# Routing the first four batches of the second expert stage inside the linear attention before it

## The chip, the cores and the metric

The program runs on one core of one Trainium2 chip. A core has a matrix engine (TensorE, PE in the rows), a vector engine (VectorE, DVE), an activation engine (ScalarE, ACT) and a general one (GpSimd, POOL), each with its own instruction queue; SyncE (SP) issues DMAs. The engines meet only at semaphores. The metric is the device time of one launch in microseconds, the median of several runs. One execution was also taken by the hardware profiler; every time of an instruction below is from that one.

## What is computed

32 sequences ("batches") of 256 tokens with 128 numbers each go through six stages: feed-forward, gated attention, feed-forward, experts, linear attention, experts. The change touches the last two. Cut to them, the reference is:

```python
# linear attention on layernorm(x), 16 heads of 64
q = elu(x @ Wq) + 1; k = elu(x @ Wk) + 1; v = x @ Wv; g = sigmoid(x @ Wg + bg)
kv = einsum('bhnd,bhne->bhde', k, v)
z = 1 / clip(einsum('bhnd,bhd->bhn', q, k.sum(-2)), 1e-6)
x = x + (einsum('bhnd,bhde->bhne', q * SCALE, kv) * z * g) @ Wo
# experts on layernorm(x): 8 experts, top 2, 76 slots for each expert and batch
logits = x @ router_w + router_b
top, idx = top_k(logits, 2); probs = softmax(top)
pos = running count of the expert among the batch's choices
einp[idx, pos] += x
o = silu((einp @ w_fc + b_fc) * (einp @ w_gate + b_gate)) @ w_proj + b_proj
x = x + 0.5 * sum(probs * o[idx, pos])
```

## The kernel before

All of x stays in SBUF as 64 tiles of 128 tokens, two for each batch. A stage is a block: each engine has a program of its own for it, and no engine begins the next stage before all have ended this one.

**The linear attention** (`lin_stage`, "lin4") is a pipeline of one turn for each batch. A turn of PE applies the heads of batch b (`apply_heads`, L1271), transposes them (L1287) and projects them out (L1295), and between these pieces does the keys (K, L1221), the products of rows and keys (XK, L1229), the queries (Q, L1240), the gates (G, L1248) and the keys and values (L1258) of batch b+1, and last the transposes of the normalised batch b+2 (L1214). Turns 0 to 30 are a hardware loop on PE, ACT and POOL; turn 31 is written out. On DVE, turns 0 to 4 are written out (each also adds rows that the expert stage before has left over), the rest are two loops: turns 5 to 27 and 28 to 30. Between the two, DVE works out mean and 1/deviation of batches 0 to 27 for the expert stage to come (`ahead.columns`, L226 to L243, on 56 tiles at once, 17 instructions of which all but two wait for the one before). A turn of DVE is: `normalise` (L261), `divide` 0 and 1 (L1496 to L1501), then key features (L1482), divides and gates (`gate`, L1510) in turn, query features (L1488) and `update` (L1516, L273). PSUM has eight banks: 0 to 3 carry K, XK, Q and G, 4 and 5 the heads and keys, 6 and 7 the transposes, the output and the transposed input.

**The expert stages** (`moe_stage`, "moe3" and "moe5") take the batches in chunks, given by a plan. For a chunk, PE goes through 8 experts, each in 4 steps of two matmuls as wide as the chunk (`up`, L1926 and L1930: 76 columns for each batch), and then one `down` (L1942), which works on blocks of 128 rows, so a chunk of 2 or 3 batches takes 2 blocks for each expert, one of 4 or 5 takes 3. A step is a slot. In the slots of a chunk the batches of the next one are routed: normalise, transpose (L1880), router (L1887), choice and masks on DVE, counts (L1894 to L1898), slots, one-hot rows (first choice on POOL, L1835, second on DVE, L2121), and `send` (L1914), 12 bfloat16 matmuls of 304 columns for each batch. The table `combine_in` says in which slots the results of the chunk before are added to x (L1766); for that POOL gathers them row by row with indirect DMAs (`gather_rows`, L1757, four for each batch), after the stores of that chunk have landed (`rows_kept`). The last chunk's rows are gathered after its last store; in moe3 they are left to the turns of lin4, in moe5 the program ends with them (`combine`, then `store`).

What differs between the two expert stages is the start. moe3 has its first chunk, of four batches, already routed: the feed-forward stage before it does this in its turns (class `RouteAhead`, whose table of lags says in which turn each step of a batch comes), so that PE begins with `up` at once. moe5 routes its first chunk, of two batches, itself, before the first slot (`in_front`), with 16 transposes of the identity on PE (`stay_warm`, L1949) ahead of the sends. The plans are:

```python
FIRST_PLAN = Plan((4, 5, 5, 5, 5, 5, 3), ...)
LAST_PLAN = Plan((2, 3, 5, 5, 5, 5, 5, 2), ...)
```

## Time and profile before

| | us |
|---|---|
| median of 3 runs | 2365.43 (2365.0 to 2366.44) |
| the profiled execution | 2363.26 |
| its span, first to last instruction | 2361.2 |
| moe3, first to last expert matmul | 498.10 to 985.36 |
| lin4, loop turn | 24.70 each |
| between lin4's last matmul and moe5's first expert matmul | 1806.15 to 1822.68 |
| moe5, first to last expert matmul | 1822.68 to 2342.23 |
| from there to the end of the span | 19.0 |

The page of the profile has PE busy 95% of the span, DVE 66%, ACT 54% and POOL 32%; the mean granted clock of PE is 0.986 of full speed. A busy matmul in a row lasts until its results are through, so that following ones overlap: what one costs is read from start to start. "Idle ... <-X" is the engine's pause before an instruction and what ended it.

### The profile page before, as it was taken

To read this page: it belongs to the slowest core of one execution; us is meant where nothing else is said; L and a number is where in the kernel's file an instruction comes from. 1 tells how busy PE (TensorE), PEld (TensorE's weight loads), DVE (VectorE), ACT (ScalarE), POOL (GpSimd) and SP (SyncE) were. 2 spreads that over 40 slices of the span, in tenths; PEclk is the share of its full clock that TensorE was granted. 3 is DMA by queue.
4 is the path that set the end of the run, shared out by engine and by line. 5 is a ranking of instruction groups with operands and counts; after the bars stand their busy time and mean duration, and the time that the engine had idled before them with its cause. 6 is when DMAs were issued, how large, how long until landed. Compare 5 with 4: busy or idle time off the path is not lost.

```text
span 2361.2 us, 45474 instructions
## 1 busy us (share of the span) xinstructions
PE 2241.9 (95%) x14426; PEld 1780.2 (75%) x14426; DVE 1563.1 (66%) x5019; ACT 1277.0 (54%) x2619; POOL 756.0 (32%) x848
## 2 busy tenths in 40 slices
PE   5989998999999999899999999999998989999996
PEld 4979987977777777776777777777776876777776
DVE  6967777876776776556655656656566666767755
ACT  4755545754444444465566666666653444444443
POOL 0402122534676665500000000000001556666754
PEclk9999999999999999999999999999999999999998
DMA  7040000000111111200000000000000001111122
GB/s 266 0 170 0 0 0 1 2 7 24 36 39 40 36 39 47 53 3 0 0 0 0 0 0 0 0 0 0 0 0 1 19 24 35 41 53 48 41 57 76
DMA packets 70833, 68.13 MB, mean 29 GB/s; under 512 B 9520, under 2 KB 58160, under 8 KB 70320
## 3 DMA queue, kind: packets, MB, share of 16 engines
...
q10 hardware_dynamic: 1344, 2.16, 0.3%
q8 instruction: 61, 1.00, 0.2%
...
## 4 chain that ended last, share of the span: by engine, by line
PE 48%; DVE 4%; issue 3%; ACT 1%; POOL 1%; DMA 0%; ACTq 0%; DVEq 0%; POOLq 0%
PE moe_bank L1942 5%; PE lin_bank L1295 5%; PE lin_bank L1221 5%; PE lin_bank L1229 5%; PE lin_bank L1248 5%; PE lin_bank L1240 5%; PE moe_bank L1926 4%; PE moe_bank L1930 4%; PE lin_bank L1271 4%; PE lin_bank L1287 3%; PE moe_bank L1914 2%; PE lin_bank L1258 1%; POOL all_landed L1757 1%; DVE moe_hot L2121 1%; DVE all_x L1766 0%
## 5 line engine op out<-in xcount | busy, mean ns | idle before, releaser
L2010 ACT ACTIVATE moe_fc<-moe_bank,all_b_fc 128x380 f32<-128x380 f32 (+3 forms) x480 | 254.1, 529 | 299.2 <-PE moe_bank L1926 293.6
L2131 DVE SCALAR_TENSOR_TENSOR moe_act<-moe_bank,all_b_moe_gate,moe_fc 128x380 f32<-128x380 f32 (+3 forms) x480 | 263.7, 552 | 172.8 <-PE moe_bank L1930 102.7
L1942 PEld LDWEIGHTS moe_bank<-all_w_proj,moe_act 128*128 128x128 f32 x2624 | 309.5, 193 | 12.9 <-issue 1.2
L1942 PE MATMUL moe_bank<-all_w_proj,moe_act 128*128 128x128 f32 x2624 | 316.5, 277 | 1.7 <-DVE moe_expert_out L2140 1.0
L1757 POOL DMA_INDIRECT all_landed<-rows_out,all_take_at x256 | 275.9, 1078 | 120.8 <-issue 118.5
L1458 POOL COPY lin_xn_ones<-lin_xn 128x254 f32<-128x254 f32 x32 | 12.8, 399 | 740.2 <-PE lin_bank L1229 739.8
L1835 POOL TENSOR_SCALAR moe_hot<-all_slot_ids,moe_slot 128x608 bf16<-128x608 f32 x116 | 210.8, 1825 | 65.5 <-issue 33.0
L2017 ACT ACTIVATE moe_act<-moe_act 128x760 f32<-128x760 f32 (+3 forms) x240 | 178.1, 742 | 97.1 <-DVE moe_act L2131 97.1
L1362 ACT ACTIVATE lin_neg<-lin_bank 128x512 f32<-128x512 f32 x256 | 151.7, 593 | 106.7 <-PE lin_bank L1221 62.7
L1271 PEld LDWEIGHTS lin_bank<-lin_kv,lin_qT 128*128 128x128 f32 x1024 | 145.3, 192 | 73.9 <-issue 54.2
L1930 PE MATMUL moe_bank<-moe_rowsT,all_w_gate 128*128 128x380 f32 (+2 forms) x512 | 174.4, 422 | 4.2 <-DVE moe_act L2131 4.2
L1926 PE MATMUL moe_bank<-moe_rowsT,all_w_fc 128*128 128x380 f32 (+2 forms) x512 | 177.3, 428 | 0.0
L1926 PE MATMUL moe_bank<-gau_rowsT,all_w_fc 128*128 128x380 f32 (+2 forms) x448 | 171.3, 464 | 1.4 <-ACTq L2022 1.4
L1930 PE MATMUL moe_bank<-gau_rowsT,all_w_gate 128*128 128x380 f32 (+2 forms) x448 | 167.6, 456 | 0.8 <-DVE moe_act L2131 0.8
L1366 ACT ACTIVATE lin_neg<-lin_neg 128x512 f32<-128x512 f32 x256 | 161.0, 630 | 7.9
L1271 PE MATMUL lin_bank<-lin_kv,lin_qT 128*128 128x130 f32 x1024 | 153.9, 278 | 8.6 <-DVE lin_heads L1501 8.3
L1390 ACT ACTIVATE lin_gate_tanh<-lin_bank,all_bg_half 128x256 f32<-128x256 f32 x256 | 103.4, 468 | 108.2 <-PE lin_bank L1248 108.1
L2140 DVE TENSOR_TENSOR moe_expert_out<-moe_bank,all_b_proj 128x384 f32<-128x384 f32 (+1 forms) x120 | 62.4, 520 | 113.4 <-PE moe_bank L1942 103.9
L1221 PE MATMUL lin_bank<-all_wk,lin_xT 128*128 128x512 f32 x256 | 132.2, 621 | 5.0 <-ACT lin_xT L1358 3.3
L1516 DVE TENSOR_TENSOR all_x<-lin_bank,all_x 128x256 f32 (+1 forms) x32 | 13.6, 424 | 179.1 <-PE lin_bank L1295 179.1
L1930 PEld LDWEIGHTS moe_bank<-moe_rowsT,all_w_gate 128*128 128x128 f32 x512 | 93.2, 190 | 48.1 <-DVE moe_act L2131 5.2
L1295 PE MATMUL lin_bank<-all_wo,lin_gated 128*128 128x128 f32 x1024 | 127.8, 278 | 0.8 <-DVE lin_gated L1510 0.8
...
## 6 DMA issues: line engine op xcount, KB each, us to landing
...
all_landed<-rows_out,all_take_at POOLq DMA_INDIRECT x256, 2.9
...
```

Of the source, the lines that this page charges most:

```text
L1221: nc.tensor.matmul(bank[j][:, :], xT[:, j // 2 * P:(j // 2 + 1) * P], k.wk[:, j % 2 * HU:(j % 2 + 1) * HU], start=True, stop=True).then_in ...
L1271: last = nc.tensor.matmul(bank[4 + n % 2][:, i * 2 * DH1:(i + 1) * 2 * DH1], qT[:, p, t * P:(t + 1) * P], kv[:, p, :], start=True, stop=True)
L1295: last = nc.tensor.matmul(bank[6][:, t * DIM:(t + 1) * DIM], gT[:, p, t * P:(t + 1) * P], k.wo[:, p, :], start=(p == 0), stop=(p == PAIRS ...
L1366: nc.scalar.activation(neg[:, j, :], neg[:, j, :], ACT.Exp, scale=-1.0).then_inc(exps.sem, 1)
L1757: nc.gpsimd.indirect_dma_start(landed[:, b % LANDED, t, h, :], None, k.rows_out, bass.IndirectOffsetOnAxis(take_at[:, i, h:h + 1], 0), bou ...
L1835: nc.gpsimd.tensor_scalar(hot[:, b % 2, t, :], k.slot_ids[:, :], slot[:, b % 2, t, 0:1], None, ALU.is_equal).then_inc(hot_first, 1)
L1926: nc.tensor.matmul(bank[FC + j % 2][:, 0:c.width], k.w_fc[:, e, j * P:(j + 1) * P], rowsT[:, c.n % 2, e, 0:c.width], start=True, stop=True ...
L1930: nc.tensor.matmul(bank[GATE + j % 2][:, 0:c.width], k.w_gate[:, e, j * P:(j + 1) * P], rowsT[:, c.n % 2, e, 0:c.width], start=True, stop= ...
L1942: last = nc.tensor.matmul(bank[OUT][:, j * DIM:(j + 1) * DIM], act_in[:, i % 2, h, j * P:(j + 1) * P], k.w_proj[:, e * MC + h, :], start=( ...
L2010: nc.scalar.activation(fc[:, j, 0:c.width], bank[FC + j % 2][:, 0:c.width], ACT.Identity, bias=k.b_fc[:, e * MC + j:e * MC + j + 1]).then_ ...
L2017: nc.scalar.activation(a, a, ACT.Silu).then_inc(act_sb, 1)
L2131: nc.vector.scalar_tensor_tensor(act_in[:, i % 2, j, 0:c.width], bank[GATE + j % 2][:, 0:c.width], k.b_moe_gate[:, e * MC + j:e * MC + j + ...
```

## The change

1. The linear attention gets a `RouteAhead` of its own for four batches. Turns 0 to 15 stay a loop, turns 16 to 30 are written out on every engine. Batch n of the four starts in turn 16 + 3n: normalise, split, transpose in that turn, copy and router one turn later, choice, masks and count two later, slots and first choice three, second choice and first send four, second send five, last landing six. The last piece is ACT's copy in turn 31.
2. In such a turn PE does its part at the end of the turn, after `transpose_x`, in banks 3 and 2, and in the middle of the next turn (`banks_read`) waits that they have been read. DVE reads the banks after `divide` 1 (`read_psum`) and does the rest after `divide` 5 (`on_vector`). ACT copies at the start of a turn; POOL works after its copy of rows. The normalised tile and two others lie in `k.landed`, which is free by then.
3. The scales for batches 0 to 3 are worked out on DVE before turn 16 (8 tiles), those of batches 4 to 27 before turn 28 (48 tiles).
4. moe5 starts like moe3: no `in_front`, no `stay_warm`. Its plan is that of moe3 but for the last chunk, whose results of the chunk before are added in slots 15, 19, 23, 27 and 31. The first chunk's rows are in `k.rows_ahead`, the others in `rowsT`.
5. The weights of the first three stages, `rowsT` of moe3 and other tiles that are no longer needed are given up after moe3, so that the new ones fit.
6. In the feed-forward stage before moe3, two reads of PSUM move from `on_vector` to `read_psum`, called right ahead of it, and signal a semaphore of their own.

```diff
+    def banks_read(self, pe, turn):
+        for what, done, per, g in [("copy0", self.xT_sb, 1, 0), ("choose", self.logits_sb, 1, 0), ("assign", self.counts_sb, 1, 0),
+                                   ("land0", self.sent_sb, 2, 0), ("land1", self.sent_sb, 2, 1)]:
+            n = self.at(what, turn)
+            if n is not None:
+                pe.wait_ge(done, per * n + g + 1)
+
+    def read_psum(self, dve, turn):
+        nc, k = self.nc, self.k
+        n = self.at("choose", turn)
+        if n is not None:
+            dve.wait_ge(self.logits_ps, n + 1)
...
+        n = self.at("assign", turn)
...
@@ lin_stage
+        room = (k.landed[:, 0, :, 0, :], k.landed[:, 0, :, 1, :], k.landed[:, 1, 0, :, :])
+        routing = RouteAhead(k, route, ahead, LINEAR_AHEAD, [(0, 1)], [(0, 4), (4, 8)],
+                             (bank[3][:, 0:SEQ], bank[2][:, 0:TILES * EXPERTS], bank[2][:, 0:TILES * TOP_K * EXPERTS], bank[3]),
+                             k.rows_ahead[:, :, :], room)
...
-                with pe.Fori(0, BATCHES - 1) as b:
+                def turn(b):
...
                     transpose_heads(b, 0)
+                    if isinstance(b, int):
+                        routing.banks_read(pe, b)
                     K(b, 1, 2)
...
                     transpose_x(b, 2)
+                    if isinstance(b, int):
+                        pe.wait_ge(g_sb.sem, g_sb.at(b, 1, 1))
+                        routing.on_tensor(pe, b)
+
+                with pe.Fori(0, LINEAR_FROM) as b:
+                    turn(b)
+                for b in range(LINEAR_FROM, BATCHES - 1):
+                    turn(b)
...
-                with pool.Fori(1, BATCHES) as b:
+                with pool.Fori(1, LINEAR_FROM + 2) as b:
                     copy_rows(b)
+                for b in range(LINEAR_FROM, BATCHES - 1):
+                    if b + 2 < BATCHES:
+                        copy_rows(b + 2)
+                    routing.on_gpsimd(pool, b)
...
                     divide(b, 1)
+                    if routes:
+                        routing.read_psum(dve, b)
...
                     divide(b, 5)
+                    if routes:
+                        routing.on_vector(dve, b)
                     gate(b, 1)
...
-                with dve.Fori(len(k.carried.batches), AHEAD // TILES) as b:
+                with dve.Fori(len(k.carried.batches), LINEAR_FROM) as b:
                     turn(b)
-                dve.wait_ge(stat.sem, stat.at(AHEAD // TILES - 1))
-                ahead.columns(dve, chain, 0, AHEAD)
-                with dve.Fori(AHEAD // TILES, BATCHES - 1) as b:
+                dve.wait_ge(stat.sem, stat.at(route - 1))
+                ahead.columns(dve, chain, 0, TILES * route)
+                for b in range(LINEAR_FROM, BATCHES - 1):
+                    if b == AHEAD // TILES:
+                        dve.wait_ge(stat.sem, stat.at(AHEAD // TILES - 1))
+                        ahead.columns(dve, chain, TILES * route, AHEAD)
                     turn(b)
@@ plans
-LAST_PLAN = Plan((2, 3, 5, 5, 5, 5, 5, 2), (9, 5, 5, 5, 5, 5, 9),
-                 (None, (14, 6), (11, 6), (11, 5), (11, 5), (11, 5), (11, 5), (20, 5)), False)
+LAST_PLAN = Plan((4, 5, 5, 5, 5, 5, 3), (5, 5, 5, 5, 5, 9), (None, (11, 5), (11, 5), (11, 5), (11, 5), (11, 5), (15, 4)))
+LINEAR_FROM = 16
+LINEAR_AHEAD = LINEAR_FROM, 3, {"norm": 0, "transpose0": 0, "split": 0, "copy0": 1, "router": 1, "choose": 2, "mask": 2, "count": 2,
+                                "assign": 3, "first": 3, "hot0": 4, "hot1": 4, "send0": 4, "land0": 5, "send1": 5, "land1": 6}
@@ moe_stage, tensor engine
-                if how.routed_ahead:
-                    for s in (xT_ps, logits_ps, count_ps):
-                        pe.sem_inc(s, OWN)
-                    pe.sem_inc(sent_ps, 2 * OWN)
-                else:
-                    for part in (transpose_x, router, count):
-                        for b in in_front:
-                            part(b)
-                    stay_warm(WARM)
-                for b in in_front:
-                    for h in range(2):
-                        send(b, h)
+                for s in (xT_ps, logits_ps, count_ps):
+                    pe.sem_inc(s, OWN)
+                pe.sem_inc(sent_ps, 2 * OWN)
@@ program
-        lin_stage(k, "lin4")
-        moe_stage(k, "moe5", LAST_PLAN, d["out"])
+            k.rows_ahead = k.sb("rows_ahead", [P, EXPERTS, LAST_PLAN.chunks[0] * CAP])
+            lin_stage(k, "lin4", LAST_PLAN.chunks[0])
+            moe_stage(k, "moe5", LAST_PLAN, d["out"])
```

On PE, between the last matmul of lin4 (L1295) and the first expert matmuls of moe5, there stands before:

```order
L1295 MATMUL lin_bank<-all_wo,lin_gated 128x128 x16
L1198 UNCONDITIONAL_BRANCH
L1872 UNCONDITIONAL_BRANCH
L1880 MATMUL moe_bank<-all_ident,moe_xn 128x128 x4
L1887 MATMUL moe_bank<-all_w_router,moe_xT 128x8 x4
...
L1949 MATMUL moe_bank<-all_ident 128x128 x16
L1914 MATMUL moe_bank<-moe_hot,moe_parts 128x304 x24
L1926 MATMUL moe_bank<-moe_rowsT,all_w_fc 128x152
```

and after the change, at the same place:

```order
L1335 MATMUL lin_bank<-all_wo,lin_gated 128x128 x16
L1238 UNCONDITIONAL_BRANCH
L1938 UNCONDITIONAL_BRANCH
L1989 MATMUL moe_bank<-moe_rows_ahead,all_w_fc 128x304
L1993 MATMUL moe_bank<-moe_rows_ahead,all_w_gate 128x304
```

The whole routing of the first chunk is gone from there, and the first expert matmuls are 304 columns wide in place of 152.

On PE, the end of a turn of lin4, after the last gate matmuls, was the end of the loop before:

```order
L1248 MATMUL lin_bank<-lin_xT,all_wg 128x256 x2
L1214 MATMUL lin_bank<-all_ident,lin_xn 128x128 x2
L1308 REGISTER_ALU
L1308 COMPARE_AND_BRANCH
```

Now it reads, for example, at the end of turns 16, 17 and 18 (rows in between left out):

```order
L1254 MATMUL lin_bank<-all_ident,lin_xn 128x128 x2
L400 MATMUL lin_bank<-all_ident,all_landed 128x128 x2
L1311 MATMUL lin_bank<-lin_kv,lin_qT 128x130 x4
...
L1254 MATMUL lin_bank<-all_ident,lin_xn 128x128 x2
L406 MATMUL lin_bank<-all_w_router,all_landed 128x8 x2
L1311 MATMUL lin_bank<-lin_kv,lin_qT 128x130 x4
...
L1254 MATMUL lin_bank<-all_ident,lin_xn 128x128 x2
L412 MATMUL lin_bank<-lin_route_mask,all_tri 128x32
L413 MATMUL lin_bank<-lin_route_mask,all_ones 128x16
L416 MATMUL lin_bank<-lin_route_mask,all_ones 128x2x8 x2
```

One piece of a batch's routing comes between the transposes of the next input and the first heads of the next turn.

On DVE, the middle of turn 18 (choice and masks) now reads as follows; before, the gate (L1510) followed the heads (L1501) directly:

```order
L1566 TENSOR_TENSOR lin_heads<-lin_bank,lin_zinv 128x256
L491 MAX lin_route_top<-lin_route_logits 128x8 x2
L494 MAX_INDEX lin_route_top_at<-lin_route_top,lin_route_logits 128x8 x2
L501 TENSOR_TENSOR all_gap_ahead<-lin_route_top 128x2
L502 CAST lin_route_top_atf<-lin_route_top_at 128x4
L503 TENSOR_TENSOR lin_route_mask<-all_iota_experts,lin_route_top_atf 128x32
L507 SCALAR_TENSOR_TENSOR lin_route_row_base<-lin_route_top_atf,all_batch_row 128x4
L1575 SCALAR_TENSOR_TENSOR lin_gated<-lin_gate_tanh,lin_bank 128x512
```

The gate of heads 4 to 7 now stands behind the routing's vector work of that turn.

## Rows read from the trace of the kernel before

**Rows 1.** Windows: length, busy of PE, PEld, DVE, ACT, POOL, granted clock, DMA.
```profile
498.10:985.36 487.26, 480.32 (x2792) 359.80 (x2792) 337.93 (x1127) 237.47 (x449) 289.22 (x286) 1.00 0.14 37
...
1822.68:2342.23 519.55, 500.09 (x3030) 382.65 (x3028) 350.57 (x1194) 250.68 (x506) 303.88 (x300) 0.99 0.16 42
...
1198.27:1618.17 419.90, 417.34 (x2757) 326.23 (x2756) 247.66 (x697) 264.06 (x528) 6.78 (x17) 1.00 0.00 0
1714.70:1744.56 29.86, 26.45 (x162) 20.10 (x163) 17.82 (x56) 15.54 (x31) 0.40 (x1) 0.94 0.00 0
```

**Rows 2.** Timeline (start, busy, instructions), PE, from lin4 to moe5's first `up`.
```profile
1802.31 3.84 PE L1295 MATMUL lin_bank<-all_wo,lin_gated 128*128 128x128 f32 x32 [0.78 <-DVE lin_gated L1510]
...
1822.68 0.42 PE L1926 MATMUL moe_bank<-moe_rowsT,all_w_fc 128*128 128x152 f32 x2
```

**Rows 3.** Timeline, DVE, the last instructions of lin4.
```profile
1806.65 0.49 DVE L273 BATCH_NORM_STATS2 all_stats<-all_x 128x6 f32<-128x128 f32 x2
```

**Rows 4.** Timeline, ACT and PE, from the feed-forward stage to moe3's first `up`.
```profile
496.70 0.41 ACT L434 COPY gau_rowsT<-ffn_bank 128x304 f32<-128x304 f32 x1 [2.16 <-PE ffn_bank L417]
...
498.10 0.75 PE L1926 MATMUL moe_bank<-gau_rowsT,all_w_fc 128*128 128x304 f32 x2 [1.44 <-ACTq L2022]
```

**Rows 5.** Timeline, POOL, the gathers after moe5's last store.
```profile
2345.28 1.13 POOL L1757 DMA_INDIRECT all_landed<-rows_out,all_take_at  x1 [5.57 <-issue]
...
2354.60 0.99 POOL L1757 DMA_INDIRECT all_landed<-rows_out,all_take_at  x1 [0.30 <-issue]
```

**Rows 6.** Timeline, PE, the seam of two loop turns of lin4.
```profile
1614.47 0.38 PE L1214 MATMUL lin_bank<-all_ident,lin_xn 128*128 128x128 f32 x2
1614.69 1.06 PE L1271 MATMUL lin_bank<-lin_kv,lin_qT 128*128 128x130 f32 x8
...
1640.60 1.98 PE L1221 MATMUL lin_bank<-all_wk,lin_xT 128*128 128x512 f32 x4 [0.15 <-ACT lin_xT L1358]
```

**Rows 7.** Timeline, PE, routing pieces among the feed-forward stage's turns.
```profile
471.02 0.51 PE L394 MATMUL ffn_bank<-all_w_router,ffn_route_xT 128*128 128x8 f32 x4
471.39 1.47 PE L680 MATMUL ffn_bank<-ffn_x_parts,all_w_signT 128*128 128x256 bf16 x12
...
478.79 0.18 PE L400 MATMUL ffn_bank<-ffn_route_mask,all_tri 128*128 128x32 bf16 x1
...
478.89 0.94 PE L417 MATMUL ffn_bank<-ffn_route_hot,ffn_route_parts 128*128 128x304 bf16 x6
479.67 1.47 PE L680 MATMUL ffn_bank<-ffn_x_parts,all_w_signT 128*128 128x256 bf16 x12
```

**Rows 8.** Timeline, DVE, a loop turn of lin4: its pauses after `divide` 5.
```profile
1625.44 0.16 DVE L1496 TENSOR_SCALAR lin_den<-lin_bank 128x4 f32<-128x4 f32 x1 [0.21 <-PE lin_bank L1271]
...
1628.90 0.16 DVE L1496 TENSOR_SCALAR lin_den<-lin_bank 128x4 f32<-128x4 f32 x1 [1.35 <-PE lin_bank L1271]
...
1640.27 0.60 DVE L261 TENSOR_SCALAR lin_xn<-all_x,all_mean,all_rstd 128x128 f32 x2 [0.52 <-issue]
```

**Rows 9.** Timeline, DVE, routing of the first chunk in front of moe5.
```profile
1810.49 0.24 DVE L2068 MAX8 moe_top<-moe_logits 128x8 f32<-128x8 f32 x2
...
1811.93 0.15 DVE L2088 SCALAR_TENSOR_TENSOR moe_row_base<-moe_top_atf,all_batch_row 128x4 f32<-128x4 f32 x1
...
1815.33 0.85 DVE L2115 SCALAR_TENSOR_TENSOR moe_hot<-all_slot_ids,moe_slot,moe_hot 128x608 bf16<-128x608 f32 x1
```

**Rows 10.** Timeline, DVE and PE, the scales ahead of turn 28 of lin4.
```profile
1713.88 0.25 DVE L226 TENSOR_TENSOR all_mean<-all_stats 128x56 f32<-128x56 f32 x1
...
1718.45 0.60 DVE L261 TENSOR_SCALAR lin_xn<-all_x,all_mean,all_rstd 128x128 f32 x2 [0.55 <-DVE all_rstd L243]
...
1719.94 0.96 PE L1271 MATMUL lin_bank<-lin_kv,lin_qT 128*128 128x130 f32 x4 [3.26 <-DVE lin_heads L1501]
```

**Rows 11.** One source line (min/median/max ns), and a group of all instructions by line (busy, mean ns).
```profile
L2131 DVE SCALAR_TENSOR_TENSOR moe_act<-moe_bank,all_b_moe_gate,moe_fc x480: 357/607/617, 499.5 to 2339.3; 128x380 f32<-128x380 f32 x107, 128x228 f32<-128x228 f32 x21, 128x152 f32<-128x152 f32 x21, 128x304 f32<-128x304 f32 x11
...
L1835 POOL TENSOR_SCALAR moe_hot<-all_slot_ids,moe_slot 128x608 bf16<-128x608 f32 x116 | 210.8, 1825 | 65.5 <-issue 33.0 <-DVE moe_slot L2101 28.5
```

292 lines of the change are left out of this document (144 added, 148 removed).

## The prediction

> **What bounds the kernel now.** I read the windows by stage first. In the loop turns of lin4 PE is busy 417.34 of 419.90 us, in moe3 480.32 of 487.26, so in these stretches the end is set by PE's own work and what other engines do costs nothing as long as it is on time. moe5 is not as dense: 500.09 of 519.55 [rows 1]. The two expert stages compute the same thing for the same 32 batches, so moe5's 32.29 us more than moe3 is the first thing to explain. The 19.77 us of it that PE is busy are the down matmuls of a chunk more (21 blocks of 128 rows in place of 20), the routing of 30 batches in the slots in place of 28, and matmuls at half clock (mean granted clock 0.99 against 1.00); the other 12.52 us are PE idle (19.46 against 6.94). Next I read the timeline at the seams. Between the last matmul of lin4, which ends at 1802.31 + 3.84 = 1806.15, and moe5's first `up` at 1822.68 lie 16.53 us [rows 2] in which PE does only the routing of two batches. The change goes for both: the seam, and the plan of moe5.
>
> **The seam.** What is left of it after the change is the end of one block and the start of the next. The trace shows this for a stage that is routed ahead: in the feed-forward stage ACT's last copy ends at 496.70 + 0.41 = 497.11 and moe3's first `up` starts at 498.10, 0.99 us later [rows 4]. In lin4 the last instruction of any weight is DVE's statistics, which end at 1806.65 + 0.49 = 1807.14 [rows 3]. ACT's last landing comes at the start of turn 31 and is long over. So the first `up` comes at 1808.13: **-14.55 us**.
>
> **moe5 itself.** Its plan becomes moe3's: chunks 4, 5, 5, 5, 5, 5, 3, the same route steps, the same lags, no work in front. I take moe3's length as it stands: 487.26 for 519.55, **-32.29 us** [rows 1]. It differs from moe3 in the last chunk alone: five combines in slots 15, 19, 23, 27, 31 in place of four (with four pieces of norm work among them) in moe3. All five stand in slots that end with a `down` on PE, so DVE's work lies beside about 1.8 us of matmuls; I count it at 0, with -1 to +1 in the range.
>
> **The tail.** After the last matmul, POOL gathers the last chunk row set by row set, and that is now three batches in place of two: 12 indirect DMAs in place of 8. The eight start at 2345.28 to 2354.60, one in 1.33 us [rows 5]; four more are **+5.3 us**. The last store grows from 256 to 384 KB. The span ends 2361.2 - 2354.60 = 6.60 us after the start of the last gather, and that holds a landing, a combine and this store; if as much as 2.7 us of it were transfer the bigger one would cost 1.36 more, if it were all fixed time nothing. I take **+0.5**.
>
> **PE work that moves into lin4.** PE has no gaps there, so it counts in full. The price of each piece is from start to start: two transposes 1614.69 - 1614.47 = 0.22 [rows 6]; the router 471.39 - 471.02 = 0.37; the counts 478.89 - 478.79 = 0.10; a send 479.67 - 478.89 = 0.78 [rows 7]. A batch is 0.22 + 0.37 + 0.10 + 2 x 0.78 = 2.25, four are +9.0. Something comes back: at each seam of two turns PE waits 0.15 us for ACT's copy of the transposed input [rows 6], and the new pieces stand right before this wait, so that it falls into them. 14 of the 15 turns end with a piece (turn 28 has none): -2.1. Together **+6.9 us**.
>
> **DVE work that moves into lin4.** It stands behind `divide` 5. From there on, DVE pauses 0.21 and then 1.35 us for PE in a loop turn [rows 8], so 1.56 us are free before the next thing PE needs is late. The heaviest turns are the choice with its masks, 1811.93 + 0.15 - 1810.49 = 1.59, and the two one-hot rows, 2 x 0.85 = 1.70 [rows 9]; what is over, 0.14, has the room of the transposes and gates that follow. I count 0, the range to +0.15 for each of 4 turns. The two new reads of PSUM (`read_psum`) stand where DVE is about to pause for ACT. PE's new waits in `banks_read` come after K of two units and two heads, some 4 us after the copy that they wait for could start; behind them on PE stand K and all that follows, but I see none late. POOL's pieces (a split, or two one-hot rows of 1.83 us [rows 11]) stand behind its copy of rows, which comes about halfway through a turn, and the next copy is due a whole turn later.
>
> **The scales.** This part costs. In turn 28 before, DVE needs 1718.45 - 0.55 - 1713.88 = 4.02 us for 17 small dependent instructions on 56 tiles; PE then stands 3.26 us for the heads [rows 10], so about 0.7 us of DVE's delay were room. The turn took 29.86 us [rows 1] in place of 419.90 / 17 = 24.70: 5.16 lost, 3.26 of them idle and the rest with the granted clock at a mean of 0.94, so part of the turn ran at 1.2 GHz. Now there are two such stops. That before turn 16 has 8 tiles: an instruction on 4 elements takes 0.15 to 0.16 [rows 9] where one on 56 takes up to 0.25, so it is between 3.0 and 4.0 us long; I take 3.2, less 0.7 of room: 2.5 us idle. That before turn 28 has 48 tiles, 3.9 us; DVE no longer loses the 0.52 us of the loop's branch [rows 8], and PE has the count and send of turn 27 to do, 0.88 less the 0.15 counted above: 3.9 - 0.7 - 0.5 - 0.7 = 2.0 us idle. Each may bring 0 to 1.8 us at the lower clock behind it; I put 1.0 and 0.6. Sum: 3.5 + 2.6 - 5.16 = **+0.9 us**. After the seam, where PE still stands 2 us behind a turn with pauses, the same: **+1.0**, from 0 to 1.8.
>
> **On the clock, one rule of the Trainium skill** (TensorE: Matmul & The Clock Gate, Part 1): how many matmuls run at the low clock is said to differ from run to run of the same kernel. The trace of one execution cannot show that. By it the three places cost anything from 0 to 5.4 us together where I put 2.6, so between 2.6 less and 2.8 more.
>
> **Sum.** -14.55 - 32.29 + 5.3 + 0.5 + 6.9 + 0.9 + 1.0 = -32.2 us. On the span of 2361.2 that is 2329.0. The profiled execution took 2363.26 and the median is 2365.43, 2.2 above it; I carry the difference over unchanged: **2333.2 us**, 1.4% less. The feed-forward stage and moe3 get the same instructions in nearly the same order: 0.
>
> **Rival 1: the routing is not covered in lin4.** If DVE's routing reached PE in full, that would be, for each batch, 0.6 for the norm, 1.6 for choice and masks, some 0.9 for the slots and 1.7 for the one-hot rows, 4.8 in all: 19 us more, 2352. More likely is a part, since a late query feature delays only the gates behind it: half of it gives about 2343. For it: the insert is up to 0.14 us larger than the pauses. Against it: those pauses are measured, and PE's queue has matmuls between each feature and its use. Chance 0.09.
>
> A second way to the same end is the port that DVE and POOL have in common. In moe3, where POOL is busy 289.22 of 487.26 us [rows 1], the DVE instruction of the kind that the turns are made of (one input in PSUM, one in SBUF) takes 607 ns in the median and 617 at most over both stages [rows 11]: no wait for POOL shows. The Trainium skill (SBUF - State Buffer, "SBUF: two separate sides") has the shared ports as an exclusive lock, but for DVE instructions with two inputs in SBUF or in a two-port mode. By that rule the features and gates are not hit, and the trace agrees. Were they held up behind the 3.65 us of POOL's one-hot rows, the turn's room of 1.2 us or so would leave 2.4 us for each of four batches: 2343 again. Chance 0.02, in the same case.
>
> **Rival 2: moe5 does not become as dense as moe3.** The 12.5 us of extra idle time in moe5 might be moe5's own, and come back in other slots. For it: nothing in its stores of x has a counterpart in moe3. Against it: its table is now moe3's. All of it back is 2345.7. Chance 0.04.
>
> **Rival 3, the other side: the written-out turns are slower than the loop.** 15 turns that PE now reads as straight code, with more waits in its queue, would have to take 32.2 / 15 = 2.15 us more each, beyond the routing, before the gain is gone; at 2.5 us each the time is 2371. Against it: moe3 is straight code and PE does 2792 matmuls in 487.26 us there, 5.7 in a microsecond, with 1.4% idle; a turn of lin4 needs 2757 / 419.90 = 6.6 [rows 1], only a little faster. From 6.6 down to 6.0 would be enough to decide it. Chance 0.04. Cases that end within 0.2%, by this or by rivals 1 and 2 together, get 0.03.
>
> **How the numbers follow.** My forecast has 0.78; its own range is 2329 to 2338, from the clock (-2.6 to +2.8), the tail (-0.5 to +0.9), the last chunk (-1 to +1) and the DVE inserts (+0.6). Rivals 1 and 2 in part reach to 2343. The range of 8 in 10 is 2328.5 to 2342. A measurement of this kernel tells 0.2% (4.7 us) from no change. Faster by more than that: 0.93; within it: 0.03; slower: 0.04.
>
> **What the changed profile would show.** moe5's first `up` about 2 us after lin4's last matmul, 304 columns wide; from there to the last `down` 487 us; 24 to 25 us from that to the end. The turns of lin4 from 17 on at 24.70 - 0.15 plus their piece: about 24.8 with transposes, 25.7 with router and send. A stop of about 2.5 us on PE in turn 16 and one of 2.0 in turn 28. DVE's pause before `divide` 7 shorter by the insert. The prediction is wrong if PE waits in `banks_read` or before the gates in every routing turn, if moe5 takes over 492 us, or if the gathers of the tail run at another pace.

## The result, and the profile after

The changed kernel takes **2328.61 us** (median of 4 runs, 2327.46 to 2329.03) where the kernel before takes 2365.22 beside it: a ratio of 0.9847, 95% interval 0.9829 to 0.9864, 36.6 us less. A second series of five runs gave 2327.14 against 2363.62, ratio 0.984 (0.9826 to 0.9855). The forecast was 2333.2, 32.2 us less, with 2328.5 to 2342 as its range. The sign, the size and nearly all terms are right, but the time is inside that range by 0.1 us only and just below the narrower one of 2329 to 2338 that the forecast gave itself. The profiled execution took 2327.46 us with a span of 2325.5, 35.7 less than before.

One thing must be known to read the experiments: in the runs of e1 to e8 every kernel, the one before included, took some 30 us longer than in the first result and in e9 to e12 (before: 2396 against 2364), and nearly all of it lies in the last chunk of the two expert stages. So these eight are read by the turns and stages in their traces and by their ratio to the kernel before in the same series, not by their time. One of e1's ten runs took 5935 us and is left out of its ratio.

Windows of the changed kernel (length, busy of PE, PEld, DVE, ACT, POOL, granted clock, DMA share, GB/s): moe3, turns 17 to 27, turn 16 and turn 28 of lin4, moe5.

```profile
499.50:986.69 487.19, 480.29 (x2792) 359.79 (x2792) 337.73 (x1127) 237.44 (x449) 289.29 (x286) 1.00 0.14 37
1447.11:1722.02 274.91, 274.91 (x1858) 216.91 (x1857) 173.86 (x529) 174.64 (x353) 21.42 (x29) 1.00 0.00 1
1418.45:1447.11 28.66, 26.77 (x166) 20.17 (x165) 17.98 (x63) 15.74 (x32) 2.49 (x5) 0.94 0.00 1
1722.02:1748.47 26.45, 24.60 (x164) 19.02 (x163) 17.96 (x60) 15.05 (x31) 3.96 (x3) 1.00 0.00 1
1814.46:2300.82 486.36, 480.00 (x2792) 359.94 (x2792) 337.39 (x1116) 237.64 (x449) 288.89 (x286) 1.00 0.17 44
```

These answer to [rows 1]. moe5 now reads like moe3: 486.36 against 487.19 us, 2792 matmul records in both. In the eleven routing turns PE is busy for all of 274.91 us, so no wait of PE for DVE's or POOL's routing shows; PE stands only in turns 16 and 28, behind the scales.

The seam, PE's timeline (start, busy, what, idle before it and what ended it):

```profile
1808.47 3.84 PE L1335 MATMUL lin_bank<-all_wo,lin_gated 128*128 128x128 f32 x32 [0.78 <-DVE lin_gated L1575]
1814.46 0.75 PE L1989 MATMUL moe_bank<-moe_rows_ahead,all_w_fc 128*128 128x304 f32 x2 [2.15 <-ACTq L2070]
```

From 1812.31 to 1814.46 are 2.15 us where [rows 2] had 16.53: 14.4 less. DVE's last statistics end at 1813.30, 1.16 us before the first `up` (0.99 was forecast):

```profile
1812.81 0.49 DVE L273 BATCH_NORM_STATS2 all_stats<-all_x 128x6 f32<-128x128 f32 x2
```

The tail, POOL's first and last gather after the last store (twelve in all):

```profile
2304.08 0.99 POOL L1826 DMA_INDIRECT all_landed<-rows_out,all_take_at  x1 [10.46 <-issue]
2318.46 1.00 POOL L1826 DMA_INDIRECT all_landed<-rows_out,all_take_at  x1 [0.30 <-issue]
```

One in (2318.46 - 2304.08) / 11 = 1.31 us, and 7.04 us from the last one's start to the end of the span. Against [rows 5] that is four more at the same pace, and 0.44 us more behind them.

The span as a sum, from the turns and stages of both profiled executions:

| place | forecast | measured | how |
|---|---|---|---|
| before moe3 | 0 | +1.4 | 498.10 to 499.50 |
| moe3 | 0 | -0.1 | 487.26 to 487.20 |
| PE's routing pieces in lin4 | +6.9 | +4.0 | see below |
| scales, turns 16 and 28 | +0.9 | +0.8 | 3.74 + 2.18 - 5.16 |
| seam | -14.55 | -14.4 | 16.53 to 2.15 |
| half clock after the seam | +1.0 | 0 | granted clock 1.00 in the last row above (not so in e9, see "The clock") |
| moe5 | -32.29 | -33.2 | 519.55 to 486.36 |
| tail | +5.8 | +5.7 | 19.0 to 24.7 |
| sum | -32.2 | -35.8 (span: -35.7) | |

### The profile page after: what moved, and what is told of

Same layout as the page of the kernel before. It is cut to its first block and busy times, and to the rows that moved or that the text cites. A ratio compares the mean times of both kernels' runs of the same rounds, so it can differ in the third digit from the quotient of the medians.

```text
span 2325.5 us, 43858 instructions
## 1 busy us (share of the span) xinstructions
PE 2220.8 (95%) x14218; PEld 1758.4 (76%) x14218; DVE 1554.7 (67%) x4986; ACT 1266.0 (54%) x2568; POOL 763.3 (33%) x852
## 3 DMA queue, kind: packets, MB, share of 16 engines
q8 instruction: 80, 1.31, 0.2%
## 5 line engine op out<-in xcount | busy, mean ns | idle before, releaser
L2059 ACT ACTIVATE moe_fc<-moe_bank,all_b_fc 128x380 f32<-128x380 f32 (+2 forms) x448 | 245.8, 549 | 298.4 <-PE moe_bank L1989 295.3
L2166 DVE SCALAR_TENSOR_TENSOR moe_act<-moe_bank,all_b_moe_gate,moe_fc 128x380 f32<-128x380 f32 (+2 forms) x448 | 257.2, 576 | 166.7 <-PE moe_bank L1993 98.3
L2005 PEld LDWEIGHTS moe_bank<-all_w_proj,moe_act 128*128 128x128 f32 x2560 | 299.6, 192 | 13.3 <-issue 2.4
L2005 PE MATMUL moe_bank<-all_w_proj,moe_act 128*128 128x128 f32 x2560 | 305.7, 276 | 2.0 <-DVE moe_expert_out L2175 2.0
L2066 ACT ACTIVATE moe_act<-moe_act 128x760 f32<-128x760 f32 (+2 forms) x224 | 174.8, 780 | 88.5 <-DVE moe_act L2166 88.5
L1904 POOL TENSOR_SCALAR moe_hot<-all_slot_ids,moe_slot 128x608 bf16<-128x608 f32 x112 | 203.7, 1826 | 45.1 <-DVE moe_slot L2143 24.4
L1989 PE MATMUL moe_bank<-moe_rowsT,all_w_fc 128*128 128x380 f32 (+1 forms) x384 | 148.9, 469 | 0.0
L1993 PE MATMUL moe_bank<-moe_rowsT,all_w_gate 128*128 128x380 f32 (+1 forms) x384 | 145.9, 462 | 0.0
L1581 DVE TENSOR_TENSOR all_x<-lin_bank,all_x 128x256 f32<-128x256 f32 (+1 forms) x32 | 13.6, 425 | 177.3 <-PE lin_bank L1335 177.3
L770 ACT ACTIVATE ffn_hT<-ffn_bank,all_b,all_alpha 128x256 f32<-128x256 f32 x248 | 119.7, 563 | 17.3 <-PE ffn_bank L716 16.6
## 6 DMA issues: line engine op xcount, KB each, us to landing
all_w_proj<-in_w_proj SPq DMA_DIRECT2D x1, 2048.0 KB, 18.5
```

The costliest lines, as they stand in the source:

```text
L1904: nc.gpsimd.tensor_scalar(hot[:, b % 2, t, :], k.slot_ids[:, :], slot[:, b % 2, t, 0:1], None, ALU.is_equal).then_inc(hot_first, 1)
L1989: nc.tensor.matmul(bank[FC + j % 2][:, 0:c.width], k.w_fc[:, e, j * P:(j + 1) * P], rows[c.n][:, e, 0:c.width], start=True, stop=True).the ...
L1993: nc.tensor.matmul(bank[GATE + j % 2][:, 0:c.width], k.w_gate[:, e, j * P:(j + 1) * P], rows[c.n][:, e, 0:c.width], start=True, stop=True) ...
L2005: last = nc.tensor.matmul(bank[OUT][:, j * DIM:(j + 1) * DIM], act_in[:, i % 2, h, j * P:(j + 1) * P], k.w_proj[:, e * MC + h, :], start=( ...
L2059: nc.scalar.activation(fc[:, j, 0:c.width], bank[FC + j % 2][:, 0:c.width], ACT.Identity, bias=k.b_fc[:, e * MC + j:e * MC + j + 1]).then_ ...
L2066: nc.scalar.activation(a, a, ACT.Silu).then_inc(act_sb, 1)
```

## The experiments

| run | median us | before, same series | ratio (95%) |
|---|---|---|---|
| e1, turns written out alone | 2391.72 | 2396.06 | 0.9985 (0.9974 to 0.9996) |
| e2, the change with the old plan | 2386.64 | 2396.06 | 0.9956 (0.9941 to 0.997) |
| e3, scales of turn 16 in a pause | 2355.16 | 2396.06 | 0.9835 (0.9818 to 0.9851) |
| e4, scales of 16 and 28 in pauses | 2355.71 | 2396.06 | 0.9828 (0.9812 to 0.9844) |
| e5, all three sets in pauses | 2352.34 | 2396.27 | 0.982 (0.9804 to 0.9836) |
| e6, choice three times | 2361.41 | 2396.27 | 0.985 (0.9832 to 0.9868) |
| e7, ACT's copy ahead of the gates | 2353.31 | 2396.27 | 0.9824 (0.9807 to 0.9841) |
| e8, five batches ahead | 2356.72 | 2396.27 | 0.9829 (0.9807 to 0.9851) |
| e9, the change again | 2327.14 | 2363.62 | 0.984 (0.9826 to 0.9855) |
| e10, e5 and e7 together | 2308.68 | 2363.62 | 0.9771 (0.9756 to 0.9786) |
| e11, e10 and e8 together | 2307.69 | 2363.62 | 0.9769 (0.9752 to 0.9785) |
| e12, fewer combines in the last chunk | 2330.92 | 2363.62 | 0.986 (0.9844 to 0.9876) |

The length of a turn of lin4, from its first heads to those of the next, in us:

| turn | before | change | e1 | e2 | e4 | e6 | e7 | e10 |
|---|---|---|---|---|---|---|---|---|
| 4 | 31.58 | 31.59 | 31.81 | 31.55 | 31.70 | 30.91 | 30.90 | 25.17 |
| 10 | 24.70 | 24.70 | 24.70 | 24.70 | 24.70 | 24.70 | 24.35 | 24.29 |
| 16 | 24.70 | 28.66 | 24.61 | 28.59 | 25.21 | 28.64 | 28.66 | 24.49 |
| 18 | 24.70 | 24.45 | 24.61 | 24.46 | 24.46 | 24.51 | 24.46 | 24.45 |
| 20 | 24.70 | 25.53 | 24.61 | 25.53 | 25.53 | 25.53 | 25.40 | 25.41 |
| 22 | 24.70 | 24.48 | 24.61 | 24.27 | 24.49 | 24.48 | 24.49 | 24.49 |
| 24 | 24.70 | 25.14 | 24.61 | 25.04 | 25.14 | 25.41 | 25.14 | 25.15 |
| 28 | 29.86 | 26.45 | 27.48 | 27.41 | 24.27 | 28.13 | 26.45 | 24.26 |
| 30 | 24.70 | 25.04 | 24.61 | 24.61 | 25.04 | 25.04 | 25.05 | 25.05 |

### e1: what writing the turns out does by itself

```diff
-                with pe.Fori(0, BATCHES - 1) as b:
+                def turn(b):
...
+                with pe.Fori(0, 16) as b:
+                    turn(b)
+                for b in range(16, BATCHES - 1):
+                    turn(b)
```

(the same on ACT, POOL and DVE, in the kernel before)

> The kernel before, with turns 16 to 30 of the linear attention written out on all engines and nothing else changed. In the changed kernel a written-out turn costs 0.3 to 0.44 us less than a loop turn plus its routing piece, where the forecast had 0.15. Theory A: this is the wait of the first K for ACT's copy, and it goes only where a routing piece fills it; then the turns here stay at 24.70 us, and the time is that of before less about 0.5 us for the loop branch of DVE ahead of turn 28. Theory B: the written-out form itself saves it; then the turns take 24.3 to 24.4 and the time is 5 to 6 us less. Theory C (rival 3 of the prediction): straight code is slower than the loop, turns over 24.8.

The turns take 24.61 us, between A (24.70) and B (24.3 to 24.4), and C falls. Writing out gives 0.09 us a turn. In the profiled execution the turns sum to 790.72 us, 1.8 less than before: 1.3 for fourteen such turns and 2.4 for turn 28, which ran with the granted clock at 1.00 here and at 0.94 before, less 1.6 in turn 31, where the clock was lower here (0.89), and 0.2 in turn 4. The idle time ahead of the first K falls from 0.15 to 0.08 us, and is not gone. First a loop turn of the kernel before, then e1:

```profile
1589.99 1.06 PE L1271 MATMUL lin_bank<-lin_kv,lin_qT 128*128 128x130 f32 x8
1591.20 1.98 PE L1221 MATMUL lin_bank<-all_wk,lin_xT 128*128 128x512 f32 x4 [0.15 <-ACT lin_xT L1358]
1593.02 0.61 PE L1271 MATMUL lin_bank<-lin_kv,lin_qT 128*128 128x130 f32 x4
```
```profile
1477.35 0.38 PE L1214 MATMUL lin_bank<-all_ident,lin_xn 128*128 128x128 f32 x2
1477.56 1.06 PE L1271 MATMUL lin_bank<-lin_kv,lin_qT 128*128 128x130 f32 x8
1478.70 1.13 PE L1221 MATMUL lin_bank<-all_wk,lin_xT 128*128 128x512 f32 x2
```

Heads end at 1478.62, K starts at 1478.70. In the change, where a piece stands ahead, K starts while the heads' last results are on their way:

```profile
1446.67 0.38 PE L1254 MATMUL lin_bank<-all_ident,lin_xn 128*128 128x128 f32 x2
1446.89 0.38 PE L400 MATMUL lin_bank<-all_ident,all_landed 128*128 128x128 f32 x2
1447.11 1.06 PE L1311 MATMUL lin_bank<-lin_kv,lin_qT 128*128 128x130 f32 x8
1448.03 1.55 PE L1261 MATMUL lin_bank<-all_wk,lin_xT 128*128 128x512 f32 x3
```

From the first heads to K are 1.21 us in the loop, 1.14 in e1 and 0.92 here. So a wait costs the shown idle time and also the overlap with the matmul ahead of it. The full price comes from turn 28 of e4, which has a piece ahead of it and none behind: 24.27 us in all, 0.43 less than a loop turn. The 0.09 of e1 are a part of it, and they are hardly the written-out form itself: e10, further down, has a loop turn without the wait, and it takes 24.29. What writing out does is mostly to make the wait shorter (1.14 for 1.21). So nearly all of the 0.43 is the price of a wait that the profile shows as 0.15.

### e2: the seam without the plan

```diff
-LAST_PLAN = Plan((4, 5, 5, 5, 5, 5, 3), (5, 5, 5, 5, 5, 9), (None, (11, 5), (11, 5), (11, 5), (11, 5), (11, 5), (15, 4)))
+LAST_PLAN = Plan((2, 3, 5, 5, 5, 5, 5, 2), (9, 5, 5, 5, 5, 5, 9),
+                 (None, (14, 6), (11, 6), (11, 5), (11, 5), (11, 5), (11, 5), (20, 5)))
```

> The changed kernel with the plan of before in moe5 (chunks 2, 3, 5, 5, 5, 5, 5, 2 and its route steps), so that two batches are routed within the linear attention. It separates the seam from the plan. Theory A: the seam gives 14.4 us, lin4 costs about 3 us (stop in turn 16, less in turn 28, the pieces of two batches), and moe5's extra idle time belongs to its short chunks, so that the body stays at 515 to 519 us: 2349 to 2352 us. Theory B: the idle time came from the cold start of the stage, with the routing of the next chunk in the slots of a narrow one unharmed: the body falls to 500 to 505 us, 2334 to 2338 us.

The times in the expectation are those of the first series, so the ratio has to answer: 0.9956, 10.4 us less, where theory A had 13 to 16. The seam is 2.1 us here as well, which is 14.4 gained, and lin4 costs 4.6 in place of 3 (the turns sum to 797.07 in place of 792.48; turn 31 alone, with the granted clock at 0.89, is 1.85 of it). moe5 without its last chunk (first row) takes 485.91 us. In the kernel before it takes 482.05 (second row), so nothing comes back there; its first two chunks (last two rows, before) have 5.55 and 8.77 us of idle time, and in e2 they are as slow, 45.57 and 66.65 us.

```profile
1829.32:2315.23 485.91, 467.87 (x2749) 351.32 (x2749) 330.05 (x1137) 232.02 (x457) 284.31 (x282) 0.99 0.15 38
```
```profile
1822.68:2304.73 482.05, 464.46 (x2750) 348.75 (x2749) 330.20 (x1135) 232.16 (x458) 283.88 (x280) 0.99 0.15 39
1822.68:1866.75 44.07, 38.52 (x309) 34.87 (x308) 26.76 (x107) 23.32 (x62) 18.30 (x18) 1.00 0.04 12
1866.75:1931.95 65.20, 56.43 (x368) 49.31 (x367) 47.84 (x184) 28.65 (x68) 37.64 (x38) 0.95 0.09 22
```

Theory A holds in its places, though the gain is smaller than it said: moe5 without its last chunk is 3.9 us longer than before, mostly in the first two chunks, whose granted clock is 0.96 and 0.92 (1.00 and 0.95 before). A seam that is gone gives its 14.4 us less what lin4 pays, and the 33 us of moe5 belong to the plan. By chunks: 44.07 + 65.20 before are 67.65 after (-41.6), the four middle ones are the same (+0.3), the sixth is 71.40 for 68.75 (+2.7), the last 43.03 for 37.50 (+5.5). Routing ahead is what makes the better plan possible, since the first chunk may then be wide; it is not itself the larger gain.

### e3, e4, e5: where the scales are worked out

```diff
+                    if in_pause:
+                        in_pause()
                     update(b)
...
-                ahead.columns(dve, chain, 0, TILES * route)
+                turn(LINEAR_FROM - 1, first_scales)
                 for b in range(LINEAR_FROM, BATCHES - 1):
-                    if b == AHEAD // TILES:
-                        dve.wait_ge(stat.sem, stat.at(AHEAD // TILES - 1))
-                        ahead.columns(dve, chain, TILES * route, AHEAD)
-                    turn(b)
+                    turn(b, other_scales if b == AHEAD // TILES else None)
```

(`first_scales` and `other_scales` hold the same wait and `ahead.columns`; e3 moves the first alone; e5 also moves `norm.columns(dve, chain, AHEAD_ATTENTION, X_TILES)` from ahead of turn 5 into it)

> The changed kernel with the scales of batches 0 to 3 worked out in turn 15, between DVE's last query feature and update, where DVE pauses 5.5 us for PE in every turn, in place of ahead of turn 16. Theory A: what the stop costs is only its place, the seam of two turns, where PE waits for DVE's heads: 3.2 us fit into the pause, turn 16 falls from 28.66 to about 24.7, and the time is 3.9 us below that of the change, 2324.7. Rival: the late update delays PE elsewhere, and the gain is under 1.5 us.

> As the run before, and also the scales of batches 4 to 27 in the same pause of turn 28 (4.0 us in 5.5). Theory A: turn 28 falls from 26.45 to 24.7 or less as well, 1.8 us more: 2322.9. Rival: 4.0 us plus the two waits are too much for the pause, update comes late, and PE waits for it in turn 29.

> The changed kernel with all three sets of scales in pauses of DVE ahead of update: those of batches 0 to 3 in turn 15, those of batches 4 to 27 in turn 28, and those of tiles 44 to 63, which both kernels work out between turns 4 and 5, in turn 5. Turn 4 takes 31.59 us, 6.4 more than the turn before it. Theory A: all three stops go, 3.9 + 1.8 + 6.4 = 12.1 us: 2316.5. Rival: part of turn 4's 6.4 us is the last combine before it and stays; then 2319 to 2321.

All three stops go, as theory A has it: turn 16 from 28.66 to 25.21 in e3 and e4 and 24.83 in e5 (24.27, its piece of 0.22 and 0.34 for the wait of K, which no piece covers there; in e10, without this wait, it is 24.49), turn 28 from 26.45 to 24.27, turn 4 from 31.59 to 25.17. DVE in turn 28 of e4: the 17 instructions run from 1753.49 on, and `update` still waits 1.81 us for PE, where it waits 5.54 in other turns of the change.

```profile
1752.28 1.30 DVE L1553 SCALAR_TENSOR_TENSOR lin_qT<-lin_bank,lin_neg 128x512 f32<-128x512 f32 x2
1753.49 0.24 DVE L226 TENSOR_TENSOR all_mean<-all_stats 128x48 f32<-128x48 f32 x1
...
1757.16 0.21 DVE L243 SCALAR_TENSOR_TENSOR all_rstd<-all_norm_tmp,all_rstd 128x48 f32<-128x48 f32 x1
1759.19 0.42 DVE L1581 TENSOR_TENSOR all_x<-lin_bank,all_x 128x256 f32<-128x256 f32 x1 [1.81 <-PE lin_bank L1335]
```

The same work costs 2.2 to 6.4 us at the seam of two turns, where PE waits for DVE's heads, and little or nothing half a turn earlier. Of the stop, 0.4 us stay in turn 16 of e3, with a wait of 0.25 us of PE for DVE's heads; it is gone in e5, and why stays open. In the sums of e1, e4 and e5 1.6 us are lost again in turn 31, which ran with a part at half clock (15.04 us in place of 13.42; granted clock 0.89 and 1.00).

### e6: how much room DVE had

```diff
+            if self.hots == 1:
+                for _ in range(2):
+                    link(last)
+                    for t in range(TILES):
+                        last = nc.vector.max(self.top[:, t, :], self.logits[:, t, :])
+                    link(last)
+                    for t in range(TILES):
+                        last = nc.vector.max_index(self.top_at[:, t, :], self.top[:, t, :], self.logits[:, t, :])
             last.then_inc(self.chosen, 1)
```

> The changed kernel with the max and max_index of the choice done three times in each of the four turns that have it, so that DVE's insert there grows by about 1.5 us, from 1.24 to 2.7. It asks how much room the change left. Theory A: the first pause behind the insert is 0.64 us in turn 18, so all but that reaches PE: 0.9 us in each of four turns, 3.4 us in all. Theory B: the gates and query features behind it have slack of their own (0.56 us more before gate 3), and the time moves by under 1.5 us. Theory C, the price of rival 1: all 1.5 us reach PE, 6 us in all.

The insert, from the first max to the gate behind it, grows from 1.24 to 2.60 us, and the turns with it (18, 21, 24, 27) from 24.45, 25.14, 25.14, 25.14 to 24.51, 25.19, 25.41, 25.19: 0.4 us together. Theory B. First the change, turn 18, then e6, the same place: the pauses of 0.64 and 0.56 us behind the insert shrink to none and 0.15, and PE loses almost nothing.

```profile
1485.73 0.16 DVE L1561 TENSOR_SCALAR lin_den<-lin_bank 128x4 f32<-128x4 f32 x1 [0.64 <-PE lin_bank L1311]
...
1487.90 0.69 DVE L1575 SCALAR_TENSOR_TENSOR lin_gated<-lin_gate_tanh,lin_bank 128x512 f32<-128x512 f32 x1 [0.56 <-PE lin_bank L1327]
```
```profile
1501.06 0.69 DVE L1583 SCALAR_TENSOR_TENSOR lin_gated<-lin_gate_tanh,lin_bank 128x512 f32<-128x512 f32 x1 [0.15 <-PE lin_bank L1335]
```

### e7: the wait itself

```diff
+                    copy_xT(b, 2, True)
                     gates(b, 1, 3)
-                    copy_xT(b, 2)
```

> The changed kernel with ACT's copy of the transposed input ahead of the last two gate activations of a turn in place of behind them, in all turns. The first K of a turn waits for this copy. Theory A: the wait costs more than the 0.15 us of idle time that the profile shows, about 0.32 us a turn; it goes in turns 0 to 15, and since the gates then come 0.4 us later, the second K, which waits for them, gets a wait of its own of 0.1 to 0.3 us: the time falls by 0 to 3 us. Theory B: the second K takes the whole wait over, and in the routing turns too, where there is none now: 2 to 8 us slower.

Better than both theories. Turns 5 to 15 take 24.35 to 24.43 us in place of 24.70, and the second K waits for nothing:

```profile
1302.80 0.38 PE L1254 MATMUL lin_bank<-all_ident,lin_xn 128*128 128x128 f32 x2
1303.02 1.06 PE L1311 MATMUL lin_bank<-lin_kv,lin_qT 128*128 128x130 f32 x8
1303.92 1.88 PE L1261 MATMUL lin_bank<-all_wk,lin_xT 128*128 128x512 f32 x4
```
```profile
1303.22 0.37 ACT L1409 COPY lin_xT<-lin_bank 128x256 f32<-128x256 f32 x1 [2.03 <-PE lin_bank L1254]
1303.49 0.85 ACT L1441 ACTIVATE lin_gate_tanh<-lin_bank,all_bg_half 128x256 f32<-128x256 f32 x2
```

ACT's gates now end at 1303.49 + 0.85 = 1304.34. The next heads start at 1305.64, so one K takes (1305.64 - 1303.92) / 4 = 0.43 us and the second starts at 1304.35: it just fits. From the first heads to the next are 2.62 us, where the loop turn above has 3.03: 0.41 less. A turn gains 0.34, since the next transposes of heads start 0.57 us after these heads in place of 0.45. The sum of the turns is 5.3 us less (791.98 against 797.29): 3.7 in turns 5 to 15, 1.0 in those routing turns whose piece did not cover the wait, and 0.7 in turn 4, which is not the copy's, for e6 and e9 have 30.91 and 30.89 there without it. Again a wait shown as 0.15 us was worth more than twice that.

### e8, e11: five batches ahead, a last chunk of two

```diff
-LAST_PLAN = Plan((4, 5, 5, 5, 5, 5, 3), (5, 5, 5, 5, 5, 9), (None, (11, 5), (11, 5), (11, 5), (11, 5), (11, 5), (15, 4)))
-LINEAR_FROM = 16
+LAST_PLAN = Plan((5, 5, 5, 5, 5, 5, 2), (5, 5, 5, 5, 5, 9), (None, (11, 5), (11, 5), (11, 5), (11, 5), (11, 5), (15, 4)))
+LINEAR_FROM = 13
```

(and the one-hot rows of the routing ahead in the free part of `landed`, since SBUF is full; e11 has this together with the edits of e10)

> The changed kernel with five batches routed ahead, from turn 13 on, and chunks 5, 5, 5, 5, 5, 5, 2 in moe5. The last chunk has two batches in place of three: four indirect gathers less in the tail, 5.2 us, and a smaller last store. Theory A: the tail falls from 24.7 to 19.2 us, the fifth batch costs lin4 2.25 less 3 x 0.3 = about 1.3 us and moves as much out of moe5's slots, so the time is 4 to 5 us below that of the change: 2324. Rival: the last chunk is too narrow (152 columns) for the five combines and 20 gathers in it, POOL's gathers of 26 us and DVE's combines come late, PE or the tail waits for them, and nothing is gained.

The tail falls to 18.9 us as forecast, and the linear attention stays (the turns sum to 796.74). The ratio, 0.9829, is not to be told from that of e5 or e7. What became of the gain is read better in e11:

> As e10, with five batches routed ahead and a last chunk of two (as in e8). In e8 the tail fell from 24.7 to 18.9 us and the linear attention did not get longer. Theory A: that adds 5.5 us to e10's gain, ratio 0.9747. Rival: the 20 gathers of 26 us in a last chunk of 37 us cost PE what the tail gives (the last chunk took 58.7 us in e8 against 59 to 63 with three batches, so it gave back nothing of its narrower matmuls there): ratio equal to e10's within 0.1%.

The rival: 0.9769 against 0.9771 for e10. The tail gives 6.3 us (18.80 for 25.09), the turns of the linear attention take 2.1 (781.44 for 779.32), and moe5 takes 6.1, so that these three are 1.9 us longer; the profiled execution is 1.0 shorter only by what lies ahead of turn 0, where the two kernels do the same. In moe5 the first chunk is 7.6 longer (five batches), the sixth 2.7 shorter, and the last, now 152 columns wide, 44.17 us where two batches took 37.50 before. There DVE waits for the gathered rows, and PE for DVE:

```profile
2261.11 1.26 DVE L1846 SCALAR_TENSOR_TENSOR all_x<-all_landed,all_prob,all_x 128x128 f32<-128x128 f32 x4 [2.22 <-DMA all_landed<-rows_out,all_take_at]
```
```profile
2263.56 0.53 PE L2004 MATMUL moe_bank<-moe_rowsT,all_w_gate 128*128 128x152 f32 x2 [2.16 <-DVE moe_act L2177]
...
2272.99 0.53 PE L2004 MATMUL moe_bank<-moe_rowsT,all_w_gate 128*128 128x152 f32 x2 [1.07 <-DVE moe_act L2177]
```

A batch's four gathers take 5.2 us of POOL, and four slots of this width are shorter than that (from one `down` to the next 4.24 us, 2264.44 to 2268.68), so each combine stands a little longer in DVE's queue and holds the products behind it. Combines from slot 11 on, five slots apart, would have more room; that was not tried.

### e9, e10: the change again, and the better version

> The changed kernel itself, on the chip of the runs that follow. Its ratio was 0.9847 (0.9829 to 0.9864) on the chip of the first result. On the chip of the last runs the last chunk of both expert stages took 13 to 20 us more in every kernel (57.8 against 44.1 us in moe3 with the same instructions), so a time there is about 2360, and the ratio should still be 0.984 to 0.987, since both kernels have two such chunks. If the change had a price of its own in that state, a wider last chunk under POOL's gathers, the ratio would be above 0.987.

0.984 (0.9826 to 0.9855): the first result holds. What the expectation calls another chip was none, since e5 to e8 ran on the same one as e9 to e12.

> The changed kernel with all three sets of scales in DVE's pauses (as in e5) and ACT's copy of the transposed input ahead of the last gates (as in e7). In those runs the turns 0 to 31 took 793.46 less 6.76 us with the third set moved, and 5.3 us less with the copy alone. Theory A: the two have different places and add up: against the change the turns lose 3.4 + 2.2 + 6.4 for the scales and 11 x 0.34 + 1.6 for the copy, 17 us in all, ratio 0.977. Rival: with the scales in the pauses DVE becomes late for the heads, and the earlier K only waits longer: 12 us, ratio 0.9795.

Theory A: 0.9771, 18.5 us less than e9 where it had 17. Its windows, turn 4, turns 5 to 15, turn 16:

```profile
1114.26:1139.44 25.18, 24.67 (x165) 19.03 (x163) 19.28 (x65) 15.54 (x31) 0.40 (x1) 1.00 0.00 0
1139.44:1406.63 267.19, 267.19 (x1785) 210.29 (x1784) 163.32 (x469) 170.95 (x341) 4.39 (x11) 1.00 0.00 0
1406.63:1431.12 24.49, 24.49 (x167) 19.33 (x166) 15.10 (x45) 15.56 (x32) 2.48 (x5) 1.00 0.00 1
```

PE has no idle time from turn 5 to turn 15, a turn takes 24.29 us, and the stops of turns 4, 16 and 28 are gone. The seam of two loop turns:

```profile
1285.20 1.06 PE L1311 MATMUL lin_bank<-lin_kv,lin_qT 128*128 128x130 f32 x8
1286.10 1.88 PE L1261 MATMUL lin_bank<-all_wk,lin_xT 128*128 128x512 f32 x4
1287.81 0.61 PE L1311 MATMUL lin_bank<-lin_kv,lin_qT 128*128 128x130 f32 x4
```

From heads to heads are 2.61 us, as in e7, where the loop turn of the kernel before has 3.03; 24.70 less 24.29 is the same 0.41. So in the loop the wait costs about 0.4 us, and a loop turn without it is within 0.03 of the written-out ones (24.27 in turn 28 of e4, 24.26 in that of e10). The turns sum to 779.32 us against 798.38 in e9 (797.29 in the first profile of the change; e9's turn 28 ran at a lower clock). At 2308.68 us this is 55 us below the kernel before and 18 below the change.

### e12: fewer gathers in the last chunk

```diff
-(11, 5), (15, 4)))
+(11, 5), (11, 10)))
```

> The changed kernel with only three of the five combines in moe5's last chunk, ten slots apart, so that POOL issues 12 gathers in three groups there in place of 20 in a row; the other eight move into the tail, which grows by 8 x 1.3 = 10.4 us. It asks where the last chunk's extra time on the second chip comes from. Theory A: from many gathers in a row: the chunk falls from 59 to 63 us to about 45, and the whole is 4 to 8 us shorter than the change on that chip (on the first chip, where the chunk took 43 us, it would be 10 us longer). Theory B: from the chunk's narrow matmuls or its place at the end of the program: it stays near 60 us and the time grows by 10 us.

This run tells nothing of its question, for two reasons: the condition it was to explain was absent (the last chunk took 43.0 us in e9), and the edit did not do what I took it to do. POOL gathers what is not combined in the chunk as soon as it is free, so there were 20 gathers in a row again, from 2265.53 to 2290.26, and the tail stayed at 24.6. The 3.8 us by which it is slower lie in that chunk (46.95 us in place of 43.02): a wait of 2.0 us of PE for DVE, and the lower clock behind it (0.96 over the chunk).

## Why the prediction was right, point by point

- **What bounds the kernel**: right. moe5's extra 32 us against moe3 were the place to look. The first chunks hold them (e2), and with moe3's plan moe5 takes moe3's time.
- **The seam**: right, 14.4 for 14.55. The last statistics of DVE are indeed what ends last: 1813.30, where PE has ended at 1812.31.
- **moe5**: -33.2 for -32.29. The one chunk that differs from moe3's is 1.1 us shorter, 43.03 against 44.11. moe3's last chunk has a PE wait of 0.82 us for DVE, in slot 19, three slots behind a combine that stands in a slot without a `down` at its end (16); in moe5's, where every combine has a `down`, there is no such wait. No run tells whether it is the slot or the norm work behind the combine. The range had -1 to +1 for this chunk, so it is just outside. Both chunks wait 1.0 us for DVE ahead of the last `down`.
- **The tail**: right, +5.7 for +5.8.
- **PE work moved into lin4**: the term that was mis-sized, +4.0 for +6.9. The pieces cost what the rows said: turns 17 to 27, 29 and 30 sum to 325.34 us; 13 turns of 24.27 are 315.51, and the 9.8 between are the pieces (8.8 forecast) and the rest of the wait where the piece ahead is too small or missing. Turn 21, with a count and a send, shows it singly: 24.27 + 0.10 + 0.78 = 25.15, measured 25.14. The step that failed is "at each seam of two turns PE waits 0.15 us ... -2.1": I took the idle time shown as the price of the wait. Of the 9.0 us of pieces 5.0 came back where I had 2.1. By e4 and e10 a turn without the wait is 0.43 and 0.41 us shorter than a loop turn, and at most 0.03 of that is the written-out form. The range had no room for this term; that the time is still inside it is luck.
- **DVE work moved into lin4**: right at 0, and with more room than forecast. I had 1.56 us free; e6 puts 2.60 us there for 0.1 us a turn. The pauses further down the turn, 0.64 and 0.56 us, are room as well, since PE's queue has matmuls between a late gate and its use.
- **The scales**: +0.8 for +0.9, partly by luck. Idle 1.89 and 1.85 us where I had 2.5 and 2.0. The first was followed by half clock (granted 0.94 in turn 16) and cost 3.74 in all for 3.5, the second was not (1.00) and cost 2.18 for 2.6. In e9 the second was as well, and turn 28 is 1.7 us longer.
- **The clock**: forecast 1.0 us after the seam, measured 0 in the first profile. In e9 it came: the first chunk of moe5 took 68.91 us with the granted clock at 0.98, where the first profile has 67.65 at 1.00, so 1.25 us. Of the nine profiled executions with this seam and four batches ahead, four (e4, e6, e7, e9) have the long chunk and five the short one, so the 0 of the first profile is chance. The rule of the Trainium skill (TensorE: Matmul & The Clock Gate, Part 1), that the number of low-clock matmuls differs from run to run, is borne out: turn 28 of the same kernel took 26.45 us in the first profile and 28.15 in e9, with the same idle time of PE (1.85 and 1.86). The row of e9 has the clock at 0.94:

```profile
1716.49:1744.64 28.15, 26.29 (x165) 19.87 (x163) 17.89 (x60) 15.06 (x31) 3.95 (x3) 0.94 0.00 1
```

- **From the profiled execution to the median**: I carried 2.2 us over from the kernel before; it was 1.15 (2327.46 to 2328.61). That is 1.1 of the 4.6 us between forecast and result, and lies within the scatter of the four runs (2327.46 to 2329.03).
- **Not in the forecast**: 1.4 us more before moe3, where the two kernels do nearly the same; the clock record has 17.0 us at the lower of the two levels there in place of 10.2. In e9 moe3 begins at 496.89, 1.2 us earlier than before, so it does not come with every execution of the change.
- **Rival 1**, routing uncovered or held up by POOL: no sign, PE is busy throughout turns 17 to 27. Its price was also too high: by e6 an insert twice as large hardly reaches PE. **Rival 2**, moe5 less dense than moe3: fell, 6.4 us idle against 6.9. **Rival 3**, straight code slower: fell, e1 has it 0.09 us a turn faster.

On the span, 2.9 us for PE's pieces, 1.0 for the clock after the seam and 0.9 for moe5, which all turned out better, less the 1.4 at the start, are 3.4 of the 3.5 us from 32.2 to 35.7.
